# Cross attention with its scores made twice and the expert layer woven into the same loop, in a decoder on one Trainium2 core

## The reference

```
# cross attention; x and ctx are (8, 256, 512)
q, k = x, ctx split into 8 heads of 32 tokens each      # (8 heads, 32, 512)
s    = einsum(q, k) / sqrt(32)                          # 512 x 512 for each head
o    = softmax(s, over the 512 key channels) @ v        # v = ctx
x    = layernorm(x + gamma * o)
# experts
gates = softmax(x @ Wr + br + bonus)                    # 8 experts
pick the two largest gates, scale them to sum 1
h     = relu(x @ Wd[e] + bd[e]) * share[e]              # 16 hidden columns an expert
x     = layernorm(x + h @ Wu + share @ bu)
```

## Time and profile before

| | |
|---|---|
| median of 3 runs | 2088.07 us (2087.61 to 2089.55) |
| the profiled execution's own time | 2083.66 us |
| its span, first to last instruction | 2081.9 us |
| first exact score of the cross attention | 1644.2 us |
| last step's scores | 1974.7 us |
| first transpose of the experts | 1993.9 us |
| mean granted TensorE clock | 0.952 of full speed |

### The profile page before, as it was taken

The page is one execution under the profiler, slowest core; times in us unless marked ns, Lnnn a source line. Parts: engine busy times, 40 slices in busy tenths (PEclk is TensorE's granted clock), DMA queues, the critical chain, the costliest instruction groups (busy, mean ns, idle before and its releaser), DMA issues. The chain is left out here.

```text
span 2081.9 us, 33021 instructions
## 1 busy us (share of the span) xinstructions
PE 1846.4 (89%) x12272; PEld 1503.4 (72%) x12272; DVE 1249.2 (60%) x2330; ACT 920.4 (44%) x2376; POOL 288.0 (14%) x347
## 2 busy tenths in 40 slices
PE   6979999999976799999999996799997498889966
PEld 5868999998964588888888985677775365555543
DVE  3446444444434565546555536788887288878847
ACT  2224333333323343333333223666666288878811
POOL 0000000000002111111111001333343111121001
PEclk9989999999997799999999998999998699999988
DMA  3122000000013231111101013000010675556234
GB/s 104 45 97 72 21 21 21 21 21 21 10 48 101 66 97 47 36 31 41 46 19 34 11 41 121 11 31 32 31 42 21 182 179 136 153 140 149 68 114 142
DMA packets 86253, 136.62 MB, mean 66 GB/s; under 512 B 9480, under 2 KB 25480, under 8 KB 86096
## 3 DMA queue, kind: packets, MB, share of 16 engines
q1 hardware_dynamic: 86096, 134.52, 22.3%
HBM read 79.88 MB, written 21.05 MB: 48 GB/s over the span
## 5 line engine op out<-in xcount | busy, mean ns | idle before, releaser
L1164 PE MATMUL yp<-ccy,toep 128*128 128x288 f32 x640 | 182.4, 436 | 19.5 <-POOL ccy L892 13.4
L1965 ACT ACTIVATE e_p<-e_s_ps,e_nb 128x512 f32<-128x512 f32 x256 | 175.0, 696 | 51.6 <-DVE e_nb L2013 49.5
L2013 DVE TENSOR_REDUCE e_nb<-e_s_ps 128x2 f32<-128x1024 f32 x128 | 155.8, 1218 | 54.3 <-PE e_s_ps L2090 53.5
L1442 ACT ACTIVATE p<-p,nb,rq 128x128 f32<-128x128 f32 (+1 forms) x256 | 137.0, 541 | 94.5 <-DVE nb L1539 94.5
L2100 PE MATMUL e_t_ps<-ident,e_p 128*128 128x128 f32 x1024 | 148.7, 284 | 24.7 <-DVE e_pT L2020 13.2
L1164 PEld LDWEIGHTS yp<-ccy,toep 128*128 128x128 f32 x640 | 126.5, 206 | 55.7 <-POOL ccy L892 14.8
L2100 PEld LDWEIGHTS e_t_ps<-ident,e_p 128*128 128x128 f32 x1024 | 120.8, 146 | 62.5 <-issue 52.9
L80 PE MATMUL q_ps<-a_xt_hi,wq_hi 128*128 128x256 f32 x512 | 151.7, 296 | 4.1 <-DVE wo_lo L112 4.1
L1062 DVE SCALAR_TENSOR_TENSOR hm<-gu_ps,us_col,sg 128x256 f32<-128x256 f32 x88 | 42.3, 481 | 182.3 <-ACT sg L971 182.3
L82 PE MATMUL q_ps<-a_xt_hi,wq_lo 128*128 128x256 f32 x512 | 146.5, 286 | 0.0
L81 PE MATMUL q_ps<-a_xt_lo,wq_hi 128*128 128x256 f32 x512 | 146.4, 286 | 0.0
(11 more groups left out here) (277 smaller groups left out, 5122.1 us busy)
## 6 DMA issues: line engine op xcount, KB each, us to landing
x_after<-n_r SPq DMA_DIRECT2D x24, 512.0 KB, 3.0
toep<-padded_kernels SPq DMA_DIRECT2D x32, 256.0 KB, 3.5
qs<-e_xh SPq DMA_DIRECT2D x64, 128.0 KB, 2.5
qs<-e_xl SPq DMA_DIRECT2D x64, 128.0 KB, 2.6
ks<-e_ch SPq DMA_DIRECT2D x64, 128.0 KB, 2.6
ks<-e_cl SPq DMA_DIRECT2D x64, 128.0 KB, 2.6
x<-x_after SPq DMA_DIRECT2D x12, 512.0 KB, 4.7
x<-in_x SPq DMA_DIRECT2D x8, 512.0 KB, 4.1
```

The costliest lines, as they stand in the source:

```text
L1164: last = pe.matmul(yp[:, lo % 2, 0:NCOL], toep[h % 2][:, (lo - li) * P:(lo - li + 1) * P], ccy[h % 2][:, li, 0:NCOL], start=(li == 0), sto ...
L1442: act.activation(p[n % 3][:, h, part[t]], p[n % 3][:, h, part[t]], ACT.Exp, bias=nb[i][:, t, h:h + 1], scale=rq[u][:, t:t + 1], accum_out= ...
L1965: act.activation(pr[i][:, a, :], s_ps[i][:, a, :], ACT.Exp, bias=nb[i][:, a:a + 1], accum_out=sums[t][:, j, q:q + 1]).then_inc(e_done, 1)
L2013: dve.tensor_reduce(nb[i][:], s_ps[i][:], AX.X, ALU.max, negate=True).then_inc(nb_done, 1)
```

## The change

The two functions become one, `l1_cross_and_experts`, with one block; x after the cross attention no longer goes through DRAM. Its parts:

- Scores are made twice. A rough pair (`rough_scores`) multiplies only the high parts, two heads in rows of 32 of the array, with queries down and keys across; DVE takes the negated maximum of it (`maxima`), 11 steps ahead (LEAD). Each half batch the maxima are turned (`turn_largest`), rounded by ACT (`round_largest`) and put by four transfers (`place_largest`) into row 96 of the stacked queries, against a row of ones in the stacked keys. The exact scores (`scores`) then come with keys down and queries across, and already less the maximum. The stack holds three parts instead of four: 24 transfers a batch instead of 32.
- `exps` therefore writes the turned probabilities directly; the transposes and their copies are gone. In place of ACT's accumulated sums, 4 more matmuls with a tile of ones a group (`d_ps`) make the sums, beside the 4 of the values.
- Sums are inverted behind transfers: ACT copies them out (`read_out`), SP lays each row of 512 over 32 partitions (`lay_sums`), DVE inverts 16 values in a partition (`invert`), SP writes them to DRAM (`keep_inverses`) and reads them back spread over all rows (`spread_inverses`); POOL scales and adds (`residual`). The very last tile is inverted in place, 512 values in a partition.
- The experts of batch b-1 and b-2 run at fixed steps of batch b. Normalizations are applied by ACT.
- At a step TensorE issues the two exact scores first, then the rough pair, then (odd steps) the values, then what else has its place there. Rough pairs, context, turned x, hidden columns and expert output share two PSUM tiles (`a_ps`) in turns.

```diff
-STEPS = HX * NQ // 2
-HALF = STEPS // 2
+STEPS = T * NQ * HT // 2
+UNITS = 2 * STEPS
+LEAD = 11
+NPT = 12
+KX = 3 * CX + 1
...
+                def stack(b):
+                    sp.wait_ge(xl_done, b + 1)
+                    sp.wait_ge(cl_done, b + 1)
+                    if b >= 2:
+                        sp.wait_ge(s_mm, UNITS * (b - 1))
+                    for j in range(HT):
+                        for dst, plan in ((qs, (xh[b % 2], xl, xh[b % 2])), (ks, (ch[b % 2], ch[b % 2], cl))):
+                            for r, src in enumerate(plan):
+                                sp.dma_start(...).then_inc(stacked[j], 16)
...
+                def place_largest(n):
+                    sp.wait_ge(nbr_done, n + 1)
+                    ...
+                    for j in range(HT):
+                        sp.dma_start(qs[b % 2][KX - 1:KX, t, j, :].bitcast(F32),
+                                     nbr[n % 2][j * CX:j * CX + 1, :].bitcast(F32)).then_inc(biased, 16)
+                def lay_sums(n):
+                    sp.wait_ge(o_read, 2 * n + 1)
+                    ...
+                    for j in range(HT):
+                        row = dsb[n % 2][j * CX:j * CX + 1, :]
+                        sp.dma_start(rcol[n % 2][j * CX:(j + 1) * CX, :], ...).then_inc(laid[n % 2], 16)
...
+                for b, step, g in steps():                                   # SP
+                    if step == 0 and 0 < b + 1 < B:
+                        stack(b + 1)
+                    if step in (2, 10) and 0 <= 2 * b - 1 + step // 8 < LAST:
+                        lay_sums(2 * b - 1 + step // 8)
+                    if step in (4, 12) and 0 <= 2 * b - 1 + step // 8 < LAST:
+                        keep_inverses(2 * b - 1 + step // 8)
+                    if step in (5, 13) and 0 <= 2 * b - 1 + step // 8 < LAST:
+                        spread_inverses(2 * b - 1 + step // 8)
+                    if step in (6, 14) and 0 <= 2 * b + 1 + step // 8 < 2 * B:
+                        place_largest(2 * b + 1 + step // 8)
...
+                for u in range(2):                                           # DVE
+                    dve.memset(ks[u][KX - 1:KX, :, :, :].bitcast(F32), 1.0).then_inc(set_up, 1)
+                take_lo(dve, 0, "cl")
+                take_lo(dve, 0, "xl")
...
+                    if 0 <= g + LEAD < PAIRS_IN_ALL:
+                        maxima(g + LEAD)
...
+                    if step in (3, 11) and 0 <= 2 * b - 1 + step // 8 < 2 * B:
+                        invert(2 * b - 1 + step // 8)
...
+                for b, step, g in steps():                                   # TensorE
+                    if 0 <= g < PAIRS_IN_ALL:
+                        scores(2 * g)
+                        scores(2 * g + 1)
+                    if 0 <= g + LEAD < PAIRS_IN_ALL:
+                        rough_scores(g + LEAD)
+                    if g == 1:
+                        pe.wait_ge(set_up, 5)
+                    if g % 2 and 0 <= (g - 3) // 2 < T * NQ * B:
+                        values((g - 3) // 2)
+                    if step == 0 and 0 <= b - 2 < B:
+                        turn_hidden(b - 2)
+                    if step == 2 and 0 <= b - 2 < B:
+                        out(b - 2)
+                    if step in (5, 13) and 0 <= 2 * b + 1 + step // 8 < 2 * B:
+                        turn_largest(2 * b + 1 + step // 8)
+                    if step == 7 and 0 < b + 1 < B:
+                        turn_context(b + 1)
+                    if step == 10 and 0 <= b - 1 < B:
+                        turn_x(b - 1)
+                    if step == 12 and 0 <= b - 1 < B:
+                        project(b - 1)
...
-        l1_cross(core, to_cross, to_experts, between[3], ctx, between[4], gamma)
-        l1_experts(core, to_experts, between[4], out, wr, br, wdn, bd, wup, bu)
+        l1_cross_and_experts(core, to_cross, between[3], ctx, out, sums, gamma, wr, br, wdn, bd, wup, bu)
```

More of the change, by code:

```diff
@@ new lines, in l1_cross_and_experts, with slot, unit, pair @@
+        place = {("context", 0): 0}
+        for at in steps():
+            for use in slot_uses(*at):
+                place[use] = len(place)
+        def slot(kind, n):
+            return a_ps[place[kind, n] % 2]
+        def unit(u):
+            b, rest = divmod(u, UNITS)
+            t, rest = divmod(rest, UNITS // 2)
+            return b, t, rest // HT, rest % HT
+        def pair(n):
+            b, rest = divmod(n, STEPS)
+            t, rest = divmod(rest, STEPS // 2)
+            return b, t, rest // 2, rest % 2
@@ new lines, in apply, with turned @@
+                def apply(b, nm, nm_done, rstd, y_done):
+                    act.wait_ge(nm_done, 2 * b + 2)
+                    for t in range(T):
+                        r = rr[b % 2][:, t, :]
+                        act.activation(r, r, ACT.Identity, bias=nm[:, t:t + 1], scale=rstd[:, t:t + 1]).then_inc(y_done, 1)
+                def turned(b):
+                    act.wait_ge(x_turned, b + 1)
+                    if b:
+                        act.wait_ge(h_mm, b)
+                    act.activation(xT[:].rearrange("p k s -> p (k s)"),
+                                   slot("x", b)[:].rearrange("p r n -> p (r n)"), ACT.Copy).then_inc(xT_done, 1)
@@ L2269, in body @@
-                def body(b, u, first, last):
-                    if not last:
-                        turned(b + 1, 1 - u)
-                    if not first:
-                        hidden(b - 1, 1 - u)
-                    exponential(b)
-                turned(0, 0)
-                over_batches(act, body, lambda b, u: hidden(b - 1, 1 - u))
+                    if b:
+                        act.wait_ge(o_mm, b)
+                    bank = slot("turned", b)
+                    act.activation(hwT[:], bank[:, 0, 0:S], ACT.Copy).then_inc(hT_done, 1)
@@ L2344, in body @@
-                def body(b, u, first, second):
-                    shift(b, u)
-                    if not first and not second:
-                        norm.apply(dve, b - 2)
-                    route(b)
-                    if not first:
-                        residual(b - 1, 1 - u)
-                dve.wait_ge(w_loaded, 64)
-                dve.tensor_scalar(bias[:, 0, 0:E], bias[:, 0, 0:E], BONUS, None, ALU.add).then_inc(prepared, 1)
-                dve.wait_ge(prepared, 3)
-                def tail(b, u):
-                    norm.apply(dve, b - 2)
-                    residual(b - 1, 1 - u)
-                    norm.apply(dve, b - 1)
@@ new lines, in rough_scores @@
+                def rough_scores(n):
+                    b, t, q, jj = pair(n)
+                    if t == q == jj == 0:
+                        pe.wait_ge(xh_done, b + 1)
+                        pe.wait_ge(ch_done, b + 1)
+                    bank = take("pair", n, nb_done, n + 1)
+                    for i in range(2):
+                        j = 2 * jj + i
+                        d = slice(j * CX, (j + 1) * CX)
+                        last = pe.matmul(bank[:, i, :], xh[b % 2][d, t, q * P:(q + 1) * P], ch[b % 2][d, t, :],
+                                         start=True, stop=True, skip_group_check=True, tile_position=(j * CX, 0))
+                    last.then_inc(a_mm, 1)
```

786 lines of the change are left out of this document (377 added, 409 removed).

## The result

| | before | changed kernel |
|---|---|---|
| median of runs on the same chip | 2088.81 us (4 runs, 2087.61 to 2090.24) | 2099.78 us (4 runs, 2098.98 to 2103.46) |
| the profiled execution's own time, its span | 2083.66, 2081.9 | 2100.3, 2098.2 |
| first exact score after POOL's first instruction of the block | 14.4 us | 38.2 us |
| from there to the last step's end | 330.7 | 378.8 |
| from there to the end | 107.0 | 46.9 |

The ratio is 1.0054, 95% interval 1.0038 to 1.0069: 11 us slower, where 2092 (+3.6) was forecast and the range reached to 2115. The block began at 1634.3 us in this execution, 4.5 later than in that of before, behind unchanged code. The two profiled executions are so compared from the block's beginning on: 463.9 us against 452.1, +11.8, near the 11.0 between the medians.

What follows compares the result with a forecast made beforehand. TensorE's order bounds the steps, with SP's queue late in each batch: start +20.5, steps +43.1 (373.8 against 330.7), tail -60, total +3.6 on 2088.07, so 2092 us; range from 2058 up to 2115.

Steps and rivals of the forecast that it cites:

- Start: Before the first exact score: memsets, low parts, stack, loads and bias rows put it at 1664.7 us, 20.5 us later.
- Two free steps: TensorE's loop of scores, rough pair, values and sums: 4.27 us for two steps, 34.2 us a batch, same rate as before.
- rival S2: Slower: rough pairs run one behind the other, 0.57 us for 0.35; +16, 2108 us; chance 0.10 together with S3.
- S3: Slower: array mode switches cost 0.25 us, not 0.14; +4 us a batch, +30, 2120 us; chance 0.10 together with S2.
- Experts and turns: On TensorE, on top of the free steps: net 7.4 us, making 41.6 us a batch if nothing else is late.
- ACT's bunch at steps 10 and 11: Step 10's chain 1.2 late, then ACT has apply, read-out, rounding and copy of turned x in a row: together +2.3 us.
- rival F: Faster: SP not on the loop, batch 45.3, 2059 to 2067 us, if laid sums land before 15.7 us; chance 0.35.
- SP, 3.3 us at step 5: Laying queues behind the stack on SP, inversion and maxima are late, TensorE loses 3.3 us at step 5's turn_largest.
- choice of experts 0.6 late: In batches 1 to 6, the choice of experts ends 0.6 us late, added to each batch's 49.5 us.
- rival S: Slower by the clock: granted clock falls once in each of six batches, 2 us each; +12, 2104 us; chance 0.13.
- Tail 47: From the last exponential to the end: 47 us in place of 107, -60, including 3.4 us for 512 reciprocals.
- second sign: Among the conditions that would make the prediction wrong: the clock falls in each batch.

Runs made afterwards that it cites:

- quarters: Changed kernel with every tile of sums inverted in place, the second half's in four quarters of 128 columns at steps 3 to 6; ratio 0.9912 to the kernel before.
- in place: Changed kernel with every tile of sums inverted where it lies, 512 values in a partition, without SP's transfers; ratio 1.0014 to the kernel before.
- sums in even steps: Changed kernel with a group's four sums matmuls moved from the odd step to the even step after it; ratio 1.0167 to the kernel before.
- stack later: Changed kernel with the next batch's stack issued as 18 transfers at step 6 and 6 at step 10, not 24 at step 0; ratio 1.0249 to the kernel before.

## Why the prediction was right or wrong

The forecast time was 8 us too low and the side was right; within it, errors of both signs cancelled.

- **Unchanged parts.** Taken as equal, and equal they are within the spread of executions: the block began between 1629.6 and 1636.8 us in the profiles of the changed kernel and the experiments, and at 1629.8 before, whose profiled execution was 4.4 us under the median of its first three runs.
- **Start, forecast 34.9 us after the block's beginning, measured 38.2.** The stack (15.5) and the low parts were right. Two memsets took 3.47 us each, not 4.25, 0.85 ns an element. The cycle an element of the Trainium skill ("VectorE: DVE Perf Modes", Zero memsets can be issued as uint32 (trn2)) had given the same 8.5 as an estimate; the measurement decides. But DVE began 0.9 late, there was 0.8 between the two for a transfer, the nine issues took 5.0 for 4.2, the rows 2.5 for 1.9, and they were usable 4.0 us after the last issue for 2.5: the largest of the misses is the landing behind loads.
- **Two free steps, forecast 4.27, measured 4.39.** The mechanism (exact score, exponential, one bank each) was right; a rough pair takes 0.43 to 0.52, between the forecast's 0.35 and rival S2's 0.57, and values with sums 1.86 for 1.9. Neither S2 nor S3 (switches at 0.25) came at its price, since two steps are 0.12 over.
- **Experts and turns 7.4 us a batch on TensorE.** Too small. With the transfers and most waits gone a batch takes 45.4, of which 8 x 4.38 = 35.0 are free steps, so 10.4 remain; the forecast had 7.4 and 2.3 for ACT's bunch at steps 10 and 11. The matmuls were sized rightly: in one batch of that kernel, from 1883.73 to 1929.13, the added groups take 7.9 us, where the terms of the forecast add up to 8.4. What failed is that waits hide them. TensorE still waits 3.0 us there, 1.8 of it for exponentials, 0.6 for the normalized x and 0.6 for the hidden columns. That 45.4 is nearly rival F's 45.3 is chance: F's sum is 41.6 on TensorE and 3.7 of being late. F's condition was half met, with landings of 1.7 to 2.2 us and issues of 0.62.
- **SP, 3.3 us at step 5 of six batches.** The step that failed in form: the wait is there twice only. TensorE, slower than forecast, comes 0.5 us after DVE is done in batch 3. The queue itself is as described (24 transfers in 15.5, laying directly behind), and the runs show it to be the floor: 24.6 us remain when TensorE is made faster, and 18.5 or 22.1 when the queue is gone. The prediction looked for the damage at the wait it knew.
- **Step 0, choice of experts 0.6 late.** Mis-sized: 0.9 to 1.9, with POOL's product on top of DVE's small operation, and a stretch of lower clock behind five of the six (0.68 in the window shown). Six times 2.7 us is what the quarters take away: the largest of the missed costs.
- **Clock.** Kept apart as rival S, at 0.13. It should have been in the forecast: each of batches 1 to 6 has a window of 4 us at 0.50 to 0.73. Comparing in place with quarters, 7.5 us of waits were worth 17.8 us in the traces; the earlier trace rows had shown the levels but not how often they would come.
- **Batch 0, 37.5 forecast, 40.8; batch 7, 39.3 forecast, 43.3.** Batch 0 ran at a mean clock of 0.85. The 4 us of batch 7 were not tried by themselves, but they go with the quarters: from its first exponential to the last it takes 41.6 us in the changed kernel and 37.3 in quarters. At its step 0 the changed kernel has a wait of 1.9 us and a window at 0.57 behind it, in quarters the wait is 0.6 with no fall.
- **Tail 47 forecast, 46.9.** Right, with its 3.3 us reciprocal; from the last exponential's end (2050.20), as the forecast counted, it is 48.0, and batch 7 is shorter by 1.1.
- **Its own signs of being wrong.** Batches 1 to 6 are 49.1 us on average, but batch 1 is 52.7, over 2 from 49.5, and the clock did fall in each of the six. By the second sign at least the forecast was wrong, though its time was near.

The sum of the errors is 3.3 + 3.3 + 4.0 - 2.4 (six batches, 294.6 for 297) - 0.1 = 8.1, the 8.2 between +3.6 and +11.8. That the six batches come so near is luck, because two errors nearly cancel: the work without stalls was 269.3 us (the kernel in quarters has it) for 6 x (41.6 + 2.3) = 263.4, and the stalls with their clock 25.3 for 33.6 (3.3 + 0.3 + 1.0 + 0.6 + 0.4 a batch).

What the change itself does with the time: the hidden experts and tail give 60 us back, the start takes 24, the batches 48. Of these 72 about 40 are not in its nature: 30 from the transfers around the reciprocal and what they drag along, 10 from the order of the start.

## What to carry to other kernels

A chain that ends just before an engine arrives shows as no wait; make the engine faster by an edit, and if the stretch keeps its length, the chain is the bound. A reciprocal of 3.3 us in each second half batch, on an engine with room, was 21 us faster in all when cut into quarters than in one piece, and 30 faster than a 0.25 us reciprocal behind transfers: price a detour by what queues behind it, on SP and on the waiting engine. And where the trace shows the granted clock falling behind waits of TensorE of 1 to 2 us, count them at more than their length: here 7.5 us of them were worth 17.8.

## What was not expected of the hardware

- After waits of 1.2 to 6.8 us on TensorE the granted clock mostly fell to 0.50 for 3 to 14 us, although TensorE was then busy all the time. Waits of 0.56 us were not followed by a fall, those of 1.2 us were in four cases of six in place, and one of 2.2 us with the sums in even steps (at 1837.12) was not. The kernel in quarters has two short stretches with windows of 0.73 to 0.84 (at 1776 and 1868 us) that follow no wait over 0.8 us. What decides was not isolated.
- A DVE product of 128x16 took 0.17 us alone and 1.15 beside a POOL product of 128x512, ending with it.
- A DVE memset of 4096 fp32 in one partition took 3.47 us; one on POOL took 3.51.
- Transfers of 2 KB landed mostly in 1.7 to 2.3 us in the changed kernel's loop and in 4.4 to 4.9 behind the nine loads of its start; with the stack later, behind three loads and a stack, they took 5 to 7 us, and DVE got them 8.5 us after the first issue.
